# Attention with a gated feed-forward layer: where the PV and denominator groups stand in TensorE's order

## The chip, the cores and the metric

The kernel runs on one NeuronCore of one Trainium2 chip. The metric is the device time in microseconds (us), a median over runs of the same program. The profiled execution has a time of its own, and the working below is made against that one.

## What is computed

The reference is a layer in two halves. The first normalizes x, makes queries from it and keys and values from a context, does masked attention in 16 heads of 32 channels, and adds the result times a gate. The second normalizes again, rounds to 8-bit floating point, multiplies by a 1024 x 1024 matrix and adds that times a second gate. Cut to what matters:

```python
# x, ctx: (8, 512, 1024); mask: (8, 1, 1024), all float32
q, k, v = Wq @ layernorm(x) + bq, Wk @ ctx + bk, Wv @ ctx + bv     # per batch, 16 heads of 32
dot  = (q.T @ k) / sqrt(32);  mask2 = mask.T * mask                # per head, 1024 x 1024
amap = softmax(mask2 * dot - (1 - mask2) * 1e6, axis=-1) * mask2
x = x + tanh(g0) * (amap @ v)
y = layernorm(x)
x = x + tanh(g1) * (fp8(y * s) / s) @ (fp8(W2 * s1) / s1)
```

## The kernel before

The kernel has two parts. The first, up to about 630 us, turns the weights, makes q, k and v for all eight batches and writes them to memory. The second, from there to the end, is the attention with the feed-forward half. The change lies in the second.

**Tiling.** The second part goes over 32 quads. A quad is four heads of one batch, 128 channels in all. The work of a quad is cut into 64 slots (NSLOT). Slot k of quad n handles head h = k % 4, block j of 128 keys and half th of 512 queries. Two score products are made for each slot. `scores` (matmul on line 701) writes a tile of 128 keys x 512 queries into one of three banks s_bank, for the exponential. `scores_for_max` (line 714) writes a tile of 128 queries x 512 keys into one of three banks x_bank, from which VectorE takes the row maxima (`maximum`, line 871). The maxima have to be known before the exponentials of their half start, so this second product runs 19 slots ahead, partly for the next quad.

**Engines.** ScalarE takes the exponential of a score tile (line 807) into probs, a ring of PR = 4 blocks with 4 heads each, and makes the copies out of PSUM. `times_v` (line 727) multiplies a block of 4 heads by v: four heads stand side by side as tiles of 32 columns in the one bank o_bank, and sixteen blocks c belong to a quad, eight to each half. GpSimd adds pairs of blocks (`add_pair`, line 970), and `denominators` (line 738) sums them over the keys with a matrix of ones into the one bank d_bank, eight groups r a quad, also as tiles of 32 columns. Each group of four such products appears as eight matmul instructions in the trace. VectorE also carries the small steps of the next stages: `negate_max` after slots 18 and 50, `invert` after slots 20 and 51, `add_ffn` (line 929) after 14 and 28, and the steps of the second normalization and the rounding, as placed by these two lines:

```python
NORM_AT = {36: 2, 37: 3, 39: 4, 40: 5, 44: 6, 45: 7, 53: 9, 56: 10, 60: 11}
NORM_AT_2 = {0: 12, 3: 13, 6: 14}
```

Steps 2 and 3 are line 908, step 6 is line 917, step 7 line 919, step 9 line 92, step 10 line 95, step 11 line 97, step 12 line 99, step 13 line 102, step 14 line 103.

**Order.** The order of work on each engine is written out by hand. TensorE's `period(n, p)` goes through the slots; in each it issues `scores` and `scores_for_max`, then, at some slots, groups of PV and denominators, and at others jobs that take a bank of x_bank as well:

```python
F_JOBS = {10: "turn_y8", 13: "ffn0", 24: "max1", 27: "ffn1", 54: "max0"}
```

Each job or tile takes the next of the three banks x_bank in turn, and waits (`wait_bank`) until the user three places before is done; a score tile waits (`s_bank_freed`) for the exponential that reads its bank. Each engine works in its written order, so a wait holds up all behind it. Two periods, of an even and an odd quad, make up the body of a loop, with the first and last quads written out.

**Chains across engines.** `invert` of the half before stands after slot 20 on VectorE. Its result goes out by `move_inv` of the SyncE queue (to memory and back, spread over partitions), behind which `load_tm` and then `set_max(n, 1)` stand in the same queue; the score of slot 32 waits for that last one.

Of the kernel before, what the change touches and what calls it, by code (L numbers as in the profile page):

```python
# [28 lines left out]
def counted(value):  # L29


    return not isinstance(value, int) or value > 0


def flamingo_gated_layer(nc, x, ctx, mask, g_xattn, g_ffn, Wq, bq, Wk, bk, Wv, bv, W2, scale, scale1, out):
# [7 lines left out]
    SJ = S // P  # L43
# [20 lines left out]
    with ctxs:  # L64
# [480 lines left out]
        with ExitStack() as at:  # L545
# [71 lines left out]
            def real(n):  # L617

                return not isinstance(n, int) or 0 <= n < NQ

            def loads_of_parity(m, p):

                return 8 * (m - p) + 16

            def maxima_at(n, k):

                return (n + 1, 1, k - XLEAD) if k >= XLEAD else (n, 0, k + NSLOT - XLEAD)
# [64 lines left out]
            with nc.Block() as block:  # L692
                @block.tensor
                def _(pe):
                    def scores(n, p, k):
                        th, j, h = k // 32, k % 32 // QH, k % QH
                        if j == 0 and h == 0:
                            pe.wait_ge(max_set, 16 * (2 * n + th + 1))
                        if counted(NSLOT * n + s_bank_freed(k) + 1):
                            pe.wait_ge(exp_done, NSLOT * n + s_bank_freed(k) + 1)  # L700
                        nc.tensor.matmul(s_bank[S_BANK_OF[k]][:, :], k_st[p][0:KS, h, j * P:(j + 1) * P],  # L701
                                         q_st[p][0:KS, th, h, :], start=True, stop=True).then_inc(scores_ready, 1)
# [6 lines left out]
                    def scores_for_max(n, k, m, p, i):  # L709
                        th, h, tc, sh = tile_of_max(i)  # L710
                        if i == 0:
                            pe.wait_ge(stacked, 16 * STACK_DMAS * (m + 1))
                        wait_bank(n, "tile", k)
                        nc.tensor.matmul(x_bank_of("tile", k)[:, :], q_st[p][0:KX, th, h, tc * P:(tc + 1) * P],  # L714
                                         k_st[p][0:KX, h, sh * HALF:(sh + 1) * HALF],
                                         start=True, stop=True).then_inc(x_ready, 1)

                    def times_v(m, p, c):
                        th, j = c // SJ, c % SJ
                        if c == 0:  # L720
                            pe.wait_ge(v_loaded[p], loads_of_parity(m, p))
                        if j == 0:
                            if counted(2 * m + th):
                                pe.wait_ge(o_copied, 2 * m + th)
                        pe.wait_ge(exp_done, NSLOT * m + QH * (c + 1))
                        for h in range(QH):
                            last = nc.tensor.matmul(o_bank[D * h:D * (h + 1), :], v_t[p][:, j, D * h:D * (h + 1)],  # L727
                                                    probs[:, c % PR, h, :], start=(j == 0), stop=(j == SJ - 1))
                        last.then_inc(pv_done, 1)

                    def denominators(m, r):
                        th, i = r // 4, r % 4
                        if i == 0:
                            if counted(2 * m + th):
                                pe.wait_ge(den_copied, 2 * m + th)
                        pe.wait_ge(pair_done, QH * SJ * m + QH * (r + 1))
                        for h in range(QH):
                            last = nc.tensor.matmul(d_bank[D * h:D * (h + 1), :], ones[:, :], pair_sum[:, r % 2, h, :],  # L738
                                                    start=(i == 0), stop=(i == 3))
                        last.then_inc(den_done, 1)  # L740

                    def turn_max(n, k, m, th):
                        pe.wait_ge(negmax_done, 3 * (2 * m + th + 1))
                        wait_bank(n, f"max{th}", k)
                        nc.tensor.matmul(x_bank_of(f"max{th}", k)[:, 0:P], neg_max[:, :], ident_r[:, :], start=True,
                                         stop=True).then_inc(max_turned, 1)

                    def turn_y8(n, k, m):
                        pe.wait_ge(norm_done, NORM_STEPS * (m + 1))
                        wait_bank(n, "turn_y8", k)  # L750
                        turned = x_bank_of("turn_y8", k)[:, :].bitcast(BF16)
                        for kc in range(KC):
                            last = nc.tensor.transpose(turned[:, kc * P:(kc + 1) * P], y8[:, kc * P:(kc + 1) * P],
                                                       ident_b[:, :])
                        last.then_inc(y8_turned, 1)

                    def ffn(n, k, m, half, kcs):
                        if 0 in kcs:
                            pe.wait_ge(y8_copied, m + 1)
                            wait_bank(n, f"ffn{half}", k)  # L760
                        for kc in kcs:
                            last = nc.tensor.matmul(x_bank_of(f"ffn{half}", k)[:, :], y8_t[:, kc, :],  # L762
                                                    w2q[:, kc, half * HALF:(half + 1) * HALF],
                                                    start=(kc == 0), stop=(kc == KC - 1))
                        if KC - 1 in kcs:
                            last.then_inc(ffn_done, 1)

                    def period(n, p):
                        for k in range(NSLOT):
                            m, odd, i = maxima_at(n, k)  # L770
                            if real(n):
                                scores(n, p, k)
                            if real(m):
                                scores_for_max(n, k, m, (p + odd) % 2, i)
                            if k % 4 == 3:
                                if k >= 7 and real(n):
                                    times_v(n, p, (k - 7) // 4)
                                if k < 7 and real(n - 1):
                                    times_v(n - 1, 1 - p, 15)
                            if k % 8 == 3:  # L780
                                if k >= 19 and real(n):
                                    denominators(n, (k - 19) // 8)
                                if k < 19 and real(n - 1):
                                    denominators(n - 1, 6 + k // 8)
                            if k == 10 and real(n - 2):
                                turn_y8(n, k, n - 2)
                            if k == 24 and real(n):
                                turn_max(n, k, n, 1)
                            if k == 54 and real(n + 1):
                                turn_max(n, k, n + 1, 0)  # L790
                            for half, at_ in ((0, 13), (1, 27)):
                                if k in (at_, at_ + 1) and real(n - 2):
                                    ffn(n, at_, n - 2, half, range(4 * (k - at_), 4 * (k - at_) + 4))

                    run(pe, period)

                @block.scalar
# [319 lines left out]
```

## Time and profile before

| | us |
|---|---|
| median of 3 runs | 2907.09 (2902.08 to 2907.44) |
| time of the profiled execution | 2906.41 |
| span in its trace | 2904.3 |
| TensorE matmul busy | 2677.0 (92%) |
| VectorE busy | 2115.2 (73%) |
| ScalarE busy | 1450.8 (50%) |
| GpSimd busy | 1720.9 (59%) |

An engine's busy time is the union of its instructions' times. Matmuls are pipelined, so the start of one to the start of the next is what a matmul costs, not its own duration. In the timeline PE is TensorE's matmuls, PEld its weight loads, DVE VectorE, ACT ScalarE, POOL GpSimd, and SPq the queue of SyncE.

### The profile page before, as it was taken

The page shows a single profiled execution, that of the slowest core. Times are in us where ns is not written, and L with a number is a line of the kernel's source. Part 1 is how long each engine was busy: PE and PEld are TensorE (multiplying, and loading weights), DVE is VectorE, ACT ScalarE, POOL GpSimd, SP SyncE. Part 2 cuts the span into 40 slices and gives each one's busy share as a digit, 9 for nine tenths or more (in the row PEclk, how much of TensorE's full clock was granted, in tenths as well). Part 3 has the DMA queues.
Part 4 walks back from the last instruction along what each step waited for, and adds up shares of the span by engine and source line. Part 5 has one row for each costly group of instructions (what it writes and reads, how often), then busy time and mean ns, then how long its engine had stood idle before and what let it go on. Part 6 is the DMA issues. An engine that isn't in the chain of part 4 may idle for free. (4 is left out here: it accounts for less than half of the span.)

```text
span 2904.3 us, 51876 instructions
## 1 busy us (share of the span) xinstructions
PE 2677.0 (92%) x13364; PEld 1389.4 (48%) x13425; DVE 2115.2 (73%) x3314; ACT 1450.8 (50%) x2574; POOL 1720.9 (59%) x1265
## 2 busy tenths in 40 slices
PE   5999999969999999999999999999999999989995
PEld 4888888734444434443444444444444344434441
DVE  5666677466787878787778787777877787878873
ACT  3333333315555555555555555555555555555553
POOL 2333334416776767666667676666766676666764
PEclk8999999969999999999999999999999999999998
DMA  6766766553333333333333333434343433333301
GB/s 211 245 220 236 248 217 231 188 105 69 76 76 77 76 77 76 77 76 77 76 77 84 75 83 77 89 76 92 76 91 74 87 76 77 76 77 76 76 27 38
DMA packets 208376, 307.54 MB, mean 106 GB/s; under 512 B 41240, under 2 KB 108888, under 8 KB 208064
## 3 DMA queue, kind: packets, MB, share of 16 engines
q1 hardware_dynamic: 195920, 265.80, 37.7%
q10 hardware_dynamic: 12144, 38.02, 3.7%
q8 instruction: 141, 2.31, 0.4%
q14 instruction: 171, 1.40, 0.2%
HBM read 200.09 MB, written 102.11 MB: 104 GB/s over the span
## 5 line engine op out<-in xcount | busy, mean ns | idle before, releaser
L970 POOL TENSOR_TENSOR pair_sum<-probs 128x512 f32<-128x512 f32 x1024 | 1354.0, 1353 | 677.0 <-ACT probs L807 677.0
L871 DVE TENSOR_REDUCE part_max<-x_bank 128x1 f32<-128x512 f32 x2048 | 1309.6, 682 | 499.8 <-PE x_bank L714 487.5
L807 ACT ACTIVATE probs<-s_bank 128x512 f32<-128x512 f32 x2048 | 1122.0, 601 | 916.9 <-PE s_bank L701 909.3
L714 PE MATMUL x_bank<-k_st,q_st 98*128 98x512 f32 x2048 | 884.8, 436 | 92.2 <-DVE part_max L871 53.9
L701 PE MATMUL s_bank<-q_st,k_st 100*128 100x512 f32 x2048 | 905.2, 444 | 54.9 <-issue 34.5
L701 PEld LDWEIGHTS s_bank<-q_st,k_st 100*128 100x128 f32 x2048 | 393.6, 193 | 547.6 <-issue 282.3
L727 PE MATMUL o_bank<-probs,v_t 128*32 128x512 f32 x4096 | 562.6, 622 | 0.0
L714 PEld LDWEIGHTS x_bank<-k_st,q_st 98*128 98x128 f32 x2048 | 398.8, 195 | 335.0 <-DVE part_max L871 225.9
L738 PE MATMUL d_bank<-pair_sum,ones 128*32 128x512 f32 x2048 | 295.2, 607 | 13.7 <-issue 12.9
L321 POOL TENSOR_TENSOR stage_lo<-stage,stage_hi 128x512 fp32r<-128x512 f32 x128 | 186.6, 1480 | 123.3 <-ACT stage_hi L391 122.8
L391 ACT ACTIVATE stage_hi<-stage 128x512 fp32r<-128x512 f32 x128 | 79.8, 632 | 192.0 <-DVE stage L475 141.8
L738 PEld LDWEIGHTS d_bank<-pair_sum,ones 128*32 128x32 f32 x2048 | 70.3, 112 | 197.4 <-issue 173.9
L309 POOL TENSOR_TENSOR rstd<-ve,neg_half 128x4 f32<-128x4 f32 x8 | 14.6, 1829 | 250.5 <-DVE ve L506 250.5
L727 PEld LDWEIGHTS o_bank<-probs,v_t 128*32 128x32 f32 x4096 | 81.5, 109 | 157.0 <-issue 102.9
L979 POOL TENSOR_TENSOR y<-o_raw,inv_b 128x1024 f32<-128x1024 f32 x32 | 76.1, 2379 | 108.6 <-DMA inv_b<-inv_scr 108.6
L762 PE MATMUL x_bank<-w2q,y_t 128*128 128x512 bf16 x451 | 119.5, 385 | 8.1 <-issue 4.9
L447 PE MATMUL bank<-c_hi,w_hi_k 128*128 128x512 f32 x256 | 100.3, 392 | 14.6 <-DVE c_lo L458 14.6
L408 ACT ACTIVATE stage<-stage,sm_now 128x512 f32<-128x512 f32 x64 | 45.4, 722 | 121.1 <-DVE stage L471 120.3
L471 DVE TENSOR_TENSOR stage<-bank,bias_v 128x512 f32<-128x512 f32 x64 | 43.5, 690 | 84.2 <-PE bank L447 83.5
L447 PE MATMUL bank<-c_lo,w_hi_k 128*128 128x512 f32 x256 | 101.6, 397 | 0.0
L447 PE MATMUL bank<-w_hi_v,c_hi 128*128 128x512 f32 x256 | 101.3, 396 | 0.0
L447 PE MATMUL bank<-w_hi_v,c_lo 128*128 128x512 f32 x256 | 101.2, 396 | 0.0
(98 smaller groups left out, 2235.1 us busy)
## 6 DMA issues: line engine op xcount, KB each, us to landing
k_st<-k_scr SPq DMA_DIRECT2D x96, 512.0 KB
q_st<-q_scr SPq DMA_DIRECT2D x192, 256.0 KB
c_raw<-in_ctx_dram ACTq DMA_DIRECT2D x32, 512.0 KB, 7.3
x_raw<-in_x_dram ACTq DMA_DIRECT2D x32, 512.0 KB, 6.0
k_scr<-stage_hi SPq DMA_DIRECT2D x64, 256.0 KB, 2.4
k_scr<-stage_lo SPq DMA_DIRECT2D x64, 256.0 KB, 2.6
v_scr<-stage SPq DMA_DIRECT2D x64, 256.0 KB, 2.7
q_scr<-stage_hi SPq DMA_DIRECT2D x64, 256.0 KB, 2.1
```

What stands on the lines that cost most here:

```text
L321: nc.gpsimd.tensor_tensor(stage_lo[:, e % STG], stage[:, g % STG], stage_hi[:, e % STG].bitcast(F32), ALU.subtract).then_inc(qk_lo, 1)
L391: nc.scalar.activation(stage_hi[:, e % STG], stage[:, g % STG], ACT.Copy).then_inc(qk_hi, 1)
L447: last = nc.tensor.matmul(acc, a, m, start=(cb == 0 and n == 0), stop=(cb == CB - 1 and n == 2))
L701: nc.tensor.matmul(s_bank[S_BANK_OF[k]][:, :], k_st[p][0:KS, h, j * P:(j + 1) * P], q_st[p][0:KS, th, h, :], start=True, stop=True).then_i ...
L714: nc.tensor.matmul(x_bank_of("tile", k)[:, :], q_st[p][0:KX, th, h, tc * P:(tc + 1) * P], k_st[p][0:KX, h, sh * HALF:(sh + 1) * HALF], sta ...
L727: last = nc.tensor.matmul(o_bank[D * h:D * (h + 1), :], v_t[p][:, j, D * h:D * (h + 1)], probs[:, c % PR, h, :], start=(j == 0), stop=(j = ...
L738: last = nc.tensor.matmul(d_bank[D * h:D * (h + 1), :], ones[:, :], pair_sum[:, r % 2, h, :], start=(i == 0), stop=(i == 3))
L762: last = nc.tensor.matmul(x_bank_of(f"ffn{half}", k)[:, :], y8_t[:, kc, :], w2q[:, kc, half * HALF:(half + 1) * HALF], start=(kc == 0), st ...
L807: nc.scalar.activation(probs[:, c % PR, h, :], s_bank[S_BANK_OF[k]][:, :], ACT.Exp).then_inc(exp_done, 1)
L871: nc.vector.tensor_reduce(part_max[:, th, sh, at:at + 1], x_bank_of("tile", k)[:, :], AX, ALU.max).then_inc(max_done, 2)
L970: nc.gpsimd.tensor_tensor(pair_sum[:, r % 2, h], probs[:, a, h], probs[:, a + 1, h], ALU.add).then_inc(pair_done, 1)
L979: nc.gpsimd.tensor_tensor(y[:, :], o_raw[:, :, :].rearrange("p a t -> p (a t)"), inv_b[:, :, :].rearrange("p a t -> p (a t)"), ALU.mult).t ...
```

## The change

At every eighth slot (k % 8 == 3), TensorE issues two PV groups and then one denominator group. Before, it issued one PV group at every fourth slot and the denominator group behind every second of them. The PV group of each even block c thereby moves four slots later, from between slots 8i+7 and 8i+8 to behind slot 8i+11; that of each odd block, and the denominators, stay at their slots. The blocks 14 and 15 of a quad are now both done in the period of the next quad. The three banks s_bank, the three banks x_bank, the ring of probs, all other engines' programs and all transfers are as before.

```diff
@@ -772,12 +772,12 @@
                                 scores(n, p, k)
                             if real(m):
                                 scores_for_max(n, k, m, (p + odd) % 2, i)
-                            if k % 4 == 3:
-                                if k >= 7 and real(n):
-                                    times_v(n, p, (k - 7) // 4)
-                                if k < 7 and real(n - 1):
-                                    times_v(n - 1, 1 - p, 15)
                             if k % 8 == 3:
+                                for c in ((k - 11) // 4, (k - 7) // 4):
+                                    if k >= 11 and real(n):
+                                        times_v(n, p, c)
+                                    if k < 11 and real(n - 1):
+                                        times_v(n - 1, 1 - p, 2 * SJ + c)
                                 if k >= 19 and real(n):
                                     denominators(n, (k - 19) // 8)
                                 if k < 19 and real(n - 1):
```

## Rows read from the trace of the kernel before

**Rows 1.** The page: busy times, and the granted TensorE clock in 40 slices.

```profile
PE 2677.0 (92%) x13364; PEld 1389.4 (48%) x13425; DVE 2115.2 (73%) x3314; ACT 1450.8 (50%) x2574; POOL 1720.9 (59%) x1265
...
PEclk8999999969999999999999999999999999999998
```

**Rows 2.** Groups of instructions, 900 to 2800 us: count, busy us, mean ns, idle before.

```profile
L871 DVE TENSOR_REDUCE part_max<-x_bank 128x1 f32<-128x512 f32 x1728 | 1106.5, 681 | 403.3 <-PE x_bank L714 392.3
```

**Rows 3.** Timeline, TensorE, slots 32 to 41 of one period: start us, duration us, instruction.

```profile
1503.04 0.49 PE L701 MATMUL s_bank<-q_st,k_st 100*128 100x512 f32 x1 [0.50 <-DMA q_st<-max_rows]
1503.37 0.39 PE L714 MATMUL x_bank<-k_st,q_st 98*128 98x512 f32 x1
...
1505.10 1.06 PE L727 MATMUL o_bank<-probs,v_t 128*32 128x512 f32 x8
1505.98 1.04 PE L738 MATMUL d_bank<-pair_sum,ones 128*32 128x512 f32 x8
1506.95 0.50 PE L701 MATMUL s_bank<-q_st,k_st 100*128 100x512 f32 x1
1507.29 0.40 PE L714 MATMUL x_bank<-k_st,q_st 98*128 98x512 f32 x1
...
1508.70 0.39 PE L714 MATMUL x_bank<-k_st,q_st 98*128 98x512 f32 x1
1509.02 1.07 PE L727 MATMUL o_bank<-probs,v_t 128*32 128x512 f32 x8
1510.02 0.50 PE L701 MATMUL s_bank<-q_st,k_st 100*128 100x512 f32 x1
...
1511.19 0.50 PE L714 MATMUL x_bank<-k_st,q_st 98*128 98x512 f32 x1 [0.19 <-DVE part_max L871]
```

**Rows 4.** Timeline, VectorE and ScalarE, in the same slots; x4 is four in one line.

```profile
1503.87 2.48 DVE L871 TENSOR_REDUCE part_max<-x_bank 128x1 f32<-128x512 f32 x4 [1.41 <-PE x_bank L714]
...
1507.49 2.07 ACT L807 ACTIVATE probs<-s_bank 128x512 f32<-128x512 f32 x4 [0.58 <-PE s_bank L701]
```

**Rows 5.** One period: us, busy of PE, PEld, DVE, ACT, POOL; clock, DMA.

```profile
1533.50:1603.90 70.40, 64.58 (x348) 28.59 (x346) 56.99 (x92) 39.44 (x72) 50.30 (x38) 1.00 0.41 87
```

**Rows 6.** TensorE's own waits, 900 to 2800 us: total us, times, longest.

```profile
PE x_bank L714 <- DVE part_max L871: 45.5, 96, 1.0
```

**Rows 7.** Groups of instructions, 900 to 2800 us: VectorE's other work.

```profile
L97 DVE TENSOR_TENSOR y<-y,big 128x1024 f32<-128x1024 f32 x27 | 57.7, 2138 | 0.0
...
L908 DVE BATCH_NORM_STATS2 st<-res 128x6 f32<-128x512 f32 x54 | 37.2, 689 | 8.1 <-POOL res L985 7.6
L103 DVE TENSOR_TENSOR y<-y,isnan 128x1024 bf16<-128x1024 bf16 x27 | 37.1, 1376 | 0.0
...
L917 DVE TENSOR_TENSOR rss<-rs,scl 128x1 f32<-128x1 f32 x27 | 29.0, 1074 | 0.0
L92 DVE TENSOR_SCALAR big<-y 128x1024 uint32<-128x1024 uint32 x27 | 27.0, 1001 | 0.0
...
L919 DVE SCALAR_TENSOR_TENSOR nb<-mv,rss 128x1 f32<-128x1 f32 x27 | 19.3, 716 | 0.0
```

**Rows 8.** Timeline, VectorE: invert, and the reductions behind it.

```profile
1349.21 0.24 DVE L896 RECIPROCAL inv_c<-den_c 128x16 f32<-128x16 f32 x1
...
1350.21 1.87 DVE L871 TENSOR_REDUCE part_max<-x_bank 128x1 f32<-128x512 f32 x3
```

**Rows 9.** Timeline, TensorE, at a turn of the loop: slots 0 and 3.

```profile
1319.55 0.49 PE L701 MATMUL s_bank<-q_st,k_st 100*128 100x512 f32 x1 [2.87 <-issue]
...
1328.42 1.93 PE L738 MATMUL d_bank<-pair_sum,ones 128*32 128x512 f32 x6 [1.94 <-issue]
```

**Rows 10.** Timeline of TensorE at slot 7 of another period, and the windows about it.

```profile
1399.92 0.80 PE L714 MATMUL x_bank<-k_st,q_st 98*128 98x512 f32 x1 [0.90 <-DVE part_max L871]
1400.64 1.94 PE L727 MATMUL o_bank<-probs,v_t 128*32 128x512 f32 x8
...
1400.00:1406.80 6.80, 6.80 (x25) 3.56 (x25) 4.84 (x7) 1.79 (x3) 3.29 (x3) 0.50 1.05 181
```

## The prediction, made before the change was run

> **What bounds the kernel now.** I read the page first: TensorE is busy 92% of the span [rows 1]. A busy TensorE is not yet the bound, so the second view is the groups of instructions in the steady attention stage (900 to 2800 us). 1728 maxima in 1900 us are 27 periods of 64 slots, 70.4 us a period [rows 2]. The third view is the timeline of eight plain slots, 32 to 39, of one period [rows 3]. The reader is to see three paces there. TensorE issues the max matmuls of three slots from 1507.29 to 1508.70, so a slot takes it 0.47 us, half of it for the score and half for the max. VectorE needs more: four reductions fill 2.48 us, of which the first shows 0.69, so the following ones come every 0.60 us [rows 4]. ScalarE does four exponentials in 2.07, one every 0.49 us [rows 4]. So between the groups of PV and denominators TensorE runs faster than VectorE, by 0.13 us a slot, and can do so only until the three banks of x_bank are full. During the groups TensorE fills no bank of x_bank and VectorE catches up. VectorE has 57.0 of 70.4 us of work in one period, TensorE 64.6 [rows 5]: TensorE is the bound on average, but the hand-over through three banks decides inside each run of slots. Direct waits of TensorE for a reduction are small today, 45.5 us in 27 periods, the longest 1.0 us [rows 6].
>
> **The part that is taken away.** The change moves one PV group of each eight slots, from between slots 7 and 8 (mod 8) to slot 11, where a PV group and a denominator group already stand. The number of instructions is the same. What it removes is one entry and one exit. From the timeline [rows 3]: the lone PV group begins at 1509.02 and the next score at 1510.02, 1.00 us; the entry costs 1509.02 - 1508.70 = 0.32 in place of 0.24, and the pair after the exit 1507.29 - 1506.95 = 0.34 in place of 0.24. The lone group is thus worth 1.00 + 0.08 + 0.10 = 1.18 us of TensorE. A group that follows another costs 1505.98 - 1505.10 = 0.88. No row shows PV behind PV; PV behind PV could cost from 0.88 (as the row of PV then denominators) to 1.00 (the row of PV then score). I take 0.87 to 0.88, since the shapes of both operands are the same in both. **The gain is 1.18 - 0.87 = 0.31 us per eight slots**, 2.5 us a period, 79 us over 32 periods, if nothing else moves.
>
> One rule bears on this. The Trainium skill, "TensorEngine Tiling (Array Packing)", Key Properties, says that changing the tiling mode drains TensorE. The rows agree in kind, with 0.3 us for the pair of changes, and by that rule alone the time would fall by the 79 us. The same page, PSUM Bottleneck, speaks against the change: tiling speeds up TensorE and not the emptying of PSUM, which may become the bound.
>
> **The part that is added.** Take a run of eight slots with the time at zero when its first score starts. X(j), the max matmul of slot j of the run, starts at 0.34 + 0.47 j if nothing holds it. Its reduction starts 0.50 us after (1503.37 to 1503.87), then one every 0.60, each 0.69 long. X(j) needs the bank of X(j-3), so it can't start before 0.34 + 0.50 + 0.69, some 0.06 for the hand-over (an estimate), and 0.60 (j-3). The wait is, rounded, 0.13 j - 0.55 + e, where e is VectorE's other work that stands before tile j-3 of the run. In a plain run e is nothing and X(7) waits 0.36 us: this alone eats the 0.31. Today the lone group stands after j = 3, and 1.18 us are added to TensorE's side for all later j, so plain runs never wait. ScalarE's side is X's form with 0.49: score(7) would be held to about 3.2 us where it starts at 3.4, so it stays covered. GpSimd's pair sums start after the exponential of the slot behind the joint group, as today, and their denominators one group later (0.87 us) hold neither add_pair up, which waits for the exponential anyway, nor the ring of four probs: times_v of an even c comes five slots before its place is written again (line by line: c at slot 4c+11, the place at 4c+16).
>
> VectorE's other work makes the waits. From its groups [rows 7], less about 0.08 of overlap each: line 97 costs 2.06, line 917 1.0, line 919 0.63, line 908 0.61, line 92 0.93, line 103 1.3; invert costs 1.0 (1349.21 to 1350.21 [rows 8]). Today's wait behind the lone group (j of 4 and more) is the same formula less 1.18, so a run adds W = 0.13 j - 0.55 + e, but no more than 1.18, and gives back 0.31: **a run's loss lies between -0.31 and +0.87**. The upper end is plain: where VectorE is late anyway, a wait fills the place of the group that leaves, and the joint group behind is 0.87 longer. The eight runs of a period, named by their first slot:
> - 4: line 103 stands after slot 6. Today the max of slot 7 already waits in front of the lone group (0.90 at 1399.92 [rows 10]) and slot 10 again; afterwards the same lateness is waited for once. Bounds as above, taken 0.0.
> - 12: X(4) takes the bank of ffn0, which add_ffn has to empty; today the lone group lies between. An estimate of 0.46, so +0.15.
> - 20: invert stands after slot 20, so X(4), slot 24, waits 1.0 - 0.03, and turn_max takes a bank behind it, some 0.2: full, +0.87.
> - 28: the score of slot 32 waits today (0.50 us at 1503.04 [rows 3]) for a chain that starts with invert at slot 20 and goes through three transfers. The chain's length from slot 20 is unchanged, so slot 32 starts where the chain ends, 0.0.
> - 36: line 908 after slots 36 and 37: X(5) waits 1.22 + 0.10 = 1.3, full; but the formula leaves 0.1 of it today, and the max of slot 41 waits more than that already (0.19 directly at 1511.19, and the loading of its weights behind the wait [rows 3]). I take 0.3 for it, +0.60.
> - 44: lines 917 and 919: X(5) 1.63 + 0.10 = 1.7, full, +0.87.
> - 52: line 92 after slot 53: X(5) 0.93 + 0.10 = 1.0, less some 0.2 at turn_max of slot 54 today: +0.55.
> - 60: line 97 in front of X(4), which is slot 0: 2.06 - 0.03 = 2.0, full, +0.87.
>
> The sum is **+3.9 us a period**. At every second period the loop turns, and TensorE sits idle for its instructions, 2.87 us at slot 0 and again in the denominators of slot 3 (1319.55 and 1328.42 [rows 9]). VectorE catches up there in both kernels, and the PV group taken out in front of that gap comes back behind it, so I count half of run 60's loss there: 3.5 us on the mean of two periods. Some 30 of the 32 periods have all this work: 30 x 3.5 = 105 us. The edges I leave at nothing.
>
> **The clock.** The granted clock is full in almost all of the stage (the row PEclk [rows 1]); besides the loop turns it fell after the wait of 0.90 us for a reduction at 1399.92, to 0.50 for 6.8 us [rows 10], in which a PV group shows 1.94 us in place of 1.06. That is the lower of the two levels, 1.2 GHz, and before it TensorE had issued only scores and waits, no group. Runs of eight slots have longer stretches of just that kind. I count five per period with about 1 us or more of waiting (slots 0, 10, 24, 41, 48), where today there is about one in two periods. A fall of 6.8 us costs at most 3.4 us and less where VectorE sets the pace. Bounds: no new fall, 0 us; a fall at each, 5 x 1.7 x 30 = 255 us. The nearest row is the one that fell, yet most waits pass without a fall, so I take one and a half falls of 1 us a period, 45 us.
>
> The sum against the profiled execution's own time, 2906.4 us (span 2904.3): 2906.4 + 105 + 45 = 3056. The median shown, 2907.1, is 0.7 above it, which I disregard.
>
> **The rivals.**
> - Heavy throttling, slower still: the long waits bring a fall of the clock nearly each time. For it: the fall of rows 10. Against: 96 direct waits in 27 periods [rows 6], and the clock's row is full nearly throughout [rows 1]. 4 falls a period at 1.5 us more: 2906 + 105 + 180 = 3191; chance 0.15.
> - The waits come at half of their size, since the extra steps of VectorE overlap better or some gaps are taken up by ffn: 2906 + 50 = 2956; chance 0.11.
> - Faster: the 0.31 us count in full, since VectorE's lateness is caught up in the joint group and isn't a wait of TensorE. This decides if the wait in an average run stays under 0.31 us, that is if VectorE's reductions follow at under 0.59 us in a run with no other work, or if the three banks free earlier than I read. For it: TensorE is busy 92% and VectorE idles a fifth. Against: five of eight runs carry 0.6 us or more of other work in their first half. 2906 - 79 = 2827; chance 0.07.
> - Nothing: the gain and the waits cancel, or the period hangs on the chain of set_max and the loop turn alone: 2907; chance 0.04. That the change doesn't do what it says is not open: the order of the groups is written out in the period.
>
> **How the numbers follow.** The forecast's chance is 0.63, with a range of its own from 2990 (waits alone, somewhat smaller) to 3120 (twice the clock's share and some more). For 8 in 10 I go down to 2950, which takes in the half-sized waits, and up to 3150, which takes a part of the heavy throttling. About 0.2% (6 us) is what a measurement of this kernel can tell from no change; faster 0.07, same 0.04, slower 0.89.
>
> **What would show it.** TensorE's groups: 24 matmuls in a row, the second PV 0.88 us behind the first. Direct waits of the max matmuls for reductions well above 45.5 us in the same number of periods, standing at slots 0, 10, 24, 40, 48 and 56, each 0.5 to 1.7 us. The slots 12 to 19 take almost the same time as today. VectorE's idle time moves into the joint groups. Granted clock below today's, with new falls inside periods. Wrong would be: those waits near 0.3 us, or a period's growth that stands in the exponentials, the pair sums or the chain to slot 32.

## The result

The changed kernel takes 3135.98 us (median of 4 runs, 3124.96 to 3148.68) against 2904.59 us beside it: a ratio of 1.080, 95% interval 1.075 to 1.086. It is slower by 231 us, where +150 us was forecast. 3136 us lies in the range of 8 in 10 (2950 to 3150), but above the forecast's own range (2990 to 3120), and is nearer to the 3191 of heavy throttling (55 us away) than to the 3056 of the forecast (80 us away). The profiled execution took 3124.96 us. TensorE, VectorE and the granted clock on the page of the changed kernel, which answer to [rows 1]:

```profile
PE 2756.7 (88%) x13364; PEld 1448.5 (46%) x13425; DVE 2111.3 (68%) x3314; ACT 1445.9 (46%) x2574; POOL 1717.8 (55%) x1265
...
PEclk8999999798899998899999988899988999899988
```

The instructions are the same ones. VectorE's busy time has not moved (2111 against 2115 us); its share has only sunk with the longer span. TensorE's busy time has grown by 80 us at the same number of matmuls, and the clock row has many more eights. Its mean is 0.923 in place of 0.958.

TensorE's own waits in the changed kernel, 900 to 2700 us (in us in total, times, longest):

```profile
PE x_bank L714 <- DVE part_max L871: 133.2, 180, 1.6
PE s_bank L701 <- issue: 42.2, 12, 3.8
PE s_bank L701 <- DMA q_st<-max_rows: 19.5, 15, 2.3
```

The direct wait for a reduction was 45.5 us in 27 periods [rows 6]; now it is 133.2 us in 23. A period is 77.8 us long, on the mean of 26, and was 70.6 in the same count. Both are read from the first max matmul of one quad to that of the next.

**A run of eight, as predicted.** The timeline of TensorE in the changed kernel, slots 44 to 51 of one period and the score behind them:

```profile
1673.10 0.50 PE L701 MATMUL s_bank<-q_st,k_st 100*128 100x512 f32 x1
...
1674.85 0.39 PE L714 MATMUL x_bank<-k_st,q_st 98*128 98x512 f32 x1
1675.27 0.50 PE L701 MATMUL s_bank<-q_st,k_st 100*128 100x512 f32 x1
1676.27 0.50 PE L714 MATMUL x_bank<-k_st,q_st 98*128 98x512 f32 x1 [0.50 <-DVE part_max L871]
1676.61 0.40 PE L701 MATMUL s_bank<-q_st,k_st 100*128 100x512 f32 x1
1677.49 0.53 PE L714 MATMUL x_bank<-k_st,q_st 98*128 98x512 f32 x1 [0.48 <-DVE part_max L871]
...
1679.67 2.68 PE L727 MATMUL o_bank<-probs,v_t 128*32 128x512 f32 x16
1682.18 1.03 PE L738 MATMUL d_bank<-pair_sum,ones 128*32 128x512 f32 x8
1683.14 0.50 PE L701 MATMUL s_bank<-q_st,k_st 100*128 100x512 f32 x1
```

VectorE in the same slots:

```profile
1673.94 0.69 DVE L871 TENSOR_REDUCE part_max<-x_bank 128x1 f32<-128x512 f32 x1 [2.19 <-PE x_bank L714]
1674.55 1.06 DVE L917 TENSOR_TENSOR rss<-rs,scl 128x1 f32<-128x1 f32 x1
1675.53 0.68 DVE L871 TENSOR_REDUCE part_max<-x_bank 128x1 f32<-128x512 f32 x1
1676.13 0.71 DVE L919 SCALAR_TENSOR_TENSOR nb<-mv,rss 128x1 f32<-128x1 f32 x1
1676.76 3.07 DVE L871 TENSOR_REDUCE part_max<-x_bank 128x1 f32<-128x512 f32 x5
```

The reader is to follow the banks. The first reduction ends at 1674.63, the step of line 917 pushes the second to 1675.53, and it ends at 1676.21: the max matmul of slot 48, which needs that bank, starts at 1676.27. Line 919 does the same to slot 49: 1677.44, 1677.49. Nothing else is late by more than 0.2 us. Then the PV groups, which cost 0.88 us each at full clock, take 1682.18 - 1679.67 = 2.51 us for two. The windows about this stretch (us; busy of PE, PEld, DVE, ACT, POOL; clock; DMA) say why:

```profile
1672.00:1678.00 6.00, 4.99 (x25) 2.35 (x17) 4.06 (x7) 4.17 (x7) 3.69 (x3) 0.99 0.01 1
1678.00:1681.30 3.30, 3.30 (x13) 1.24 (x15) 3.10 (x9) 1.68 (x4) 1.29 (x2) 0.51 0.00 0
1681.50:1688.00 6.50, 5.73 (x31) 2.89 (x24) 4.19 (x7) 3.30 (x7) 3.65 (x3) 1.00 0.17 49
```

Right behind the two waits the clock is at its lower level, 1.2 GHz, and the largest group falls into it. With the clock up, the same joint group of the same kernel, here in slot 59, is 1.74 us for the two PV groups and 2.72 until the next score:

```profile
1688.66 1.92 PE L727 MATMUL o_bank<-probs,v_t 128*32 128x512 f32 x16
1690.40 1.04 PE L738 MATMUL d_bank<-pair_sum,ones 128*32 128x512 f32 x8
1691.38 0.50 PE L701 MATMUL s_bank<-q_st,k_st 100*128 100x512 f32 x1
```

**Run by run.** From the first score of each run to that of the next, the mean of 26 periods, in us:

| run of slots | before | changed | difference | predicted |
|---|---|---|---|---|
| 4 to 11 | 9.35 | 10.37 | +1.02 | 0.0 |
| 12 to 19 | 8.74 | 8.84 | +0.10 | +0.15 |
| 20 to 27 | 8.42 | 9.36 | +0.94 | +0.87 |
| 28 to 35 | 8.89 | 9.49 | +0.60 | 0.0 |
| 36 to 43 | 7.91 | 8.76 | +0.85 | +0.60 |
| 44 to 51 | 7.89 | 10.05 | +2.16 | +0.87 |
| 52 to 59 | 7.54 | 8.25 | +0.71 | +0.55 |
| 60 to 3 | 11.59 | 12.52 | +0.93 | half of 0.87 |
| sum | 70.3 | 77.6 | +7.3 | +3.5, and 1.5 for the clock |

Thirty-one periods of 7.3 us are 226 of the 231 us.

### The profile page after: what moved, and what is told of

Its sections match the earlier page's. It is cut to its first block and busy times, and to the rows that moved or that the text cites. A ratio compares the mean times of both kernels' runs of the same rounds, so it can differ in the third digit from the quotient of the medians.

```text
span 3123.2 us, 51890 instructions
## 1 busy us (share of the span) xinstructions
PE 2756.7 (88%) x13364; PEld 1448.5 (46%) x13425; DVE 2111.3 (68%) x3314; ACT 1445.9 (46%) x2574; POOL 1717.8 (55%) x1265
## 5 line engine op out<-in xcount | busy, mean ns | idle before, releaser
L714 PE MATMUL x_bank<-k_st,q_st 98*128 98x512 f32 x2048 | 920.2, 453 | 220.6 <-DVE part_max L871 179.5
L714 PEld LDWEIGHTS x_bank<-k_st,q_st 98*128 98x128 f32 x2048 | 408.8, 200 | 522.2 <-DVE part_max L871 390.1
L727 PE MATMUL o_bank<-probs,v_t 128*32 128x512 f32 x4096 | 598.1, 710 | 0.0
L701 PEld LDWEIGHTS s_bank<-q_st,k_st 100*128 100x128 f32 x2048 | 403.4, 197 | 374.3 <-issue 256.5
L738 PE MATMUL d_bank<-pair_sum,ones 128*32 128x512 f32 x2048 | 277.7, 599 | 2.8 <-issue 1.8
L727 PEld LDWEIGHTS o_bank<-probs,v_t 128*32 128x32 f32 x4096 | 120.1, 123 | 300.9 <-issue 191.5
L813 ACT ACTIVATE o_raw<-o_bank 128x512 f32<-128x512 f32 x64 | 38.3, 598 | 149.7 <-PE o_bank L727 149.7
L447 PE MATMUL bank<-c_hi,w_lo_k 128*128 128x512 f32 x256 | 101.6, 397 | 0.0
L447 PE MATMUL bank<-x_hi,w_lo_q 128*128 128x512 f32 x256 | 101.3, 396 | 0.0
```

The lines of the kernel that those rows point to most:

```text
L447: last = nc.tensor.matmul(acc, a, m, start=(cb == 0 and n == 0), stop=(cb == CB - 1 and n == 2))
```

## The experiments

Each was timed beside the kernel before, whose median was 2898.7 to 2899.9 us there. Numbers by slot or by run of slots are means over the same 26 periods as in the table above.

### Is it the pair of PV groups?

Two PV groups stay together, and the denominators stand alone between. TensorE then changes as often between the two kinds of matmul as before. In the first form the denominators come four slots later, and ScalarE's copies of them with them:

```diff
                             if k % 8 == 3:
                                 for c in ((k - 11) // 4, (k - 7) // 4):
...
-                                if k >= 19 and real(n):
-                                    denominators(n, (k - 19) // 8)
-                                if k < 19 and real(n - 1):
-                                    denominators(n - 1, 6 + k // 8)
+                            if k % 8 == 7:
+                                if k >= 23 and real(n):
+                                    denominators(n, (k - 23) // 8)
+                                if k < 23 and real(n - 1):
+                                    denominators(n - 1, 6 + k // 8)
```

> The two PV groups stay together at slots k % 8 == 3, as in the changed kernel, but the denominator group stands alone at k % 8 == 7 (four slots later than before, and the two copies of its bank on ScalarE also four slots later, after slots 16 and 48). So TensorE enters and leaves the groups as often as in the kernel before, while PV stands behind PV as in the changed one. Theory (runs of eight slots without a group are what costs): runs are four slots again, VectorE catches up twice in eight slots, so the time is near the kernel before, 2905 to 2960 us, with few falls of the clock; by the rows 1.4 us a period more at most, since the short group is 0.1 us shorter and the denominators come later. Rival (two PV groups behind each other are slow in themselves, on their one bank): well above 3000. Rival (number of changes between the two tilings is all that counts): 2905, the same as before.

Measured: 3029.7 us, ratio 1.043 (1.039 to 1.046). No theory named this. The trace shows a cause that lies in the edit and not in the pair, at least for a part. With the denominators later, GpSimd's next pair sums wait for them, and run at another time:

```profile
1644.91 5.01 POOL L971 TENSOR_TENSOR pair_sum<-probs 128x512 f32<-128x512 f32 x4 [5.62 <-PE d_bank L738]
...
1647.51 1.21 DVE L881 TENSOR_TENSOR row_max<-part_max 128x16 f32<-128x16 f32 x1
1648.75 1.21 DVE L886 TENSOR_SCALAR neg_max<-row_max 128x16 fp32r<-128x16 f32 x1
```

The two small steps of `negate_max` take 1.21 us each under the pair sums; in the changed kernel they take 0.18 and 0.17. The run of slots 52 to 59, with the second of the two `negate_max` just before it, takes 11.00 us, in place of 7.54 before and 8.25 in the changed kernel. Run 36 to 43 is longer too (9.54 in place of 7.91), and that was not followed up. So the second form puts the denominators four slots earlier instead, where no chain starts later:

```diff
+                            if k % 8 == 7:
+                                if k >= 15 and real(n):
+                                    denominators(n, (k - 15) // 8)
+                                if k < 15 and real(n - 1):
+                                    denominators(n - 1, 7)
```

> As the run with the denominators apart, but four slots earlier than in the kernel before instead of later: two PV groups at k % 8 == 3, the denominator group alone at k % 8 == 7, all copies where they were. No chain starts later than before. Theory (what costs is the run of eight slots without a group): the time is that of the kernel before, 2885 to 2930 us, the max matmuls wait no more than there, and the clock falls as seldom. Rival (PV behind PV is slow in itself): 3000 or more, with the second PV group more than 0.88 us behind the first. Rival (the loss of the earlier run with denominators apart came from the pair of PV groups, not from its later copies): 3000 again.

Measured: 2932.6 us, ratio 1.012 (1.009 to 1.014), mean clock 0.960: just above the theory's 2930 us and far from both rivals' 3000. The kernel's groups:

```profile
1513.73 1.92 PE L727 MATMUL o_bank<-probs,v_t 128*32 128x512 f32 x16
1515.59 0.50 PE L701 MATMUL s_bank<-q_st,k_st 100*128 100x512 f32 x1
...
1517.66 1.06 PE L738 MATMUL d_bank<-pair_sum,ones 128*32 128x512 f32 x8
1518.66 0.50 PE L701 MATMUL s_bank<-q_st,k_st 100*128 100x512 f32 x1
```

Two PV groups cost 1.86 us until the next score, as PV and denominators do (1.85 in [rows 3]). Seven of the eight runs are within 0.1 us of the kernel before. The eighth, that of slots 28 to 35, is 1.3 us longer in the periods behind a turn of the loop, mostly at slot 31, behind which the next score waits for the chain of set_max (22.4 us in total in place of 11.4). The cause is the one found for run 28 of the changed kernel, further below. PV behind PV is not what costs.

### How much is the clock?

The score matmul of the slots in which TensorE waits long is issued several times into its own bank, so that the waits are filled and nothing else changes:

```diff
+                    FILL = {0: 5, 10: 4, 24: 3, 40: 2, 41: 2, 48: 3, 49: 2, 56: 3}
...
-                        nc.tensor.matmul(s_bank[S_BANK_OF[k]][:, :], k_st[p][0:KS, h, j * P:(j + 1) * P],
-                                         q_st[p][0:KS, th, h, :], start=True, stop=True).then_inc(scores_ready, 1)
+                        for _ in range(FILL.get(k, 0) + 1):
+                            last = nc.tensor.matmul(s_bank[S_BANK_OF[k]][:, :], k_st[p][0:KS, h, j * P:(j + 1) * P],
+                                                    q_st[p][0:KS, th, h, :], start=True, stop=True)
+                        last.then_inc(scores_ready, 1)
```

> The changed kernel, in which the score matmul of slots 0, 10, 24, 40, 41, 48, 49 and 56 is issued several times over (5, 4, 3, 2, 2, 3, 2 and 3 times more, 0.24 us each) into its own bank, the last one counting. The repeats fill most of the waits for VectorE that stand at these slots: 24 more matmuls, 5.7 us more of TensorE work a period. Theory (half of the loss is the clock that falls after long waits): the falls vanish for the most part, granted clock back from 0.92 to about 0.95, and although TensorE has more to do the time falls from 3136 to 3020 to 3080 us. Rival (the waits are the whole loss, and the half clock costs nothing because VectorE sets the pace there): 3136 to 3180 us. Rival (the clock falls because groups are rare, not because TensorE waits): granted clock stays at 0.92, time 3140 or more.

Measured: 2992.6 us (1.031, 1.028 to 1.034), 143 us less than the changed kernel, with 24 more matmuls in every period. The mean clock is 0.966, above that of the kernel before. The trace's record of the clock has 17 stretches at the lower level in the attention stage, where the changed kernel has 88 and the kernel before 22. Slots 48 to 51 in this kernel, and the groups behind them:

```profile
1626.27 1.20 PE L704 MATMUL s_bank<-q_st,k_st 100*128 100x512 f32 x4
1627.30 0.47 PE L718 MATMUL x_bank<-k_st,q_st 98*128 98x512 f32 x1
1627.61 0.87 PE L704 MATMUL s_bank<-q_st,k_st 100*128 100x512 f32 x3
1628.52 0.50 PE L718 MATMUL x_bank<-k_st,q_st 98*128 98x512 f32 x1
...
1630.14 1.92 PE L731 MATMUL o_bank<-probs,v_t 128*32 128x512 f32 x16
1631.88 1.04 PE L742 MATMUL d_bank<-pair_sum,ones 128*32 128x512 f32 x8
```

The max matmul of slot 49 is 1.22 us behind that of slot 48 in both kernels: VectorE sets that time, filled or not. But the PV groups behind take 1.74 us in place of 2.51. So the theory held, and the effect is larger than was expected (3020 to 3080 us): some 143 of the 231 us came with the fallen clock, and 88 us are left for the waits, where 105 had been predicted. The falls inside periods are gone altogether: from 900 to 2700 us all 13 stretches at the lower level start in slots 63 to 3, about a turn of the loop, where 45 of the changed kernel's 67 start elsewhere, 26 of them in slots 43 to 51 and 15 in slots 10 and 11. And run by run the filled kernel is longer than the kernel before by -0.01, 0.11, 0.87, -0.16, 0.47, 0.86, 0.71 and 0.13 us (in the order of the table), 3.0 us in all: close to the column that was predicted without the clock. The split is a rough one: the repeats also cost where no wait covers them, the filled kernel has fewer falls than the kernel before, and TensorE's waits for instructions changed a little (33.1 us in place of 42.2).

### Pace of the reductions, or the long steps between them?

Three pairs, each an order of before and the changed order with the same part made light. First all of it: reductions, rounding steps, statistics, add_ffn and pair sums on 64 columns.

```diff
+            LT = 64
...
-                        nc.vector.tensor_reduce(part_max[:, th, sh, at:at + 1], x_bank_of("tile", k)[:, :], AX,
+                        nc.vector.tensor_reduce(part_max[:, th, sh, at:at + 1], x_bank_of("tile", k)[:, 0:LT], AX,
...
-                            ins = f8_step(step - 9, y[:, :], big[:, :], y8[:, :], isnan[:, :])
+                            ins = f8_step(step - 9, y[:, 0:LT], big[:, 0:LT], y8[:, 0:LT], isnan[:, 0:LT])
```

> The order of before, with VectorE and GpSimd made light: the reductions read 64 of 512 columns, the rounding steps, the statistics and add_ffn 64 columns of their 512 or 1024, the pair sums 64 columns. This leaves out most of the maxima, of the second half's arithmetic and of the denominators. It is the base for the next run. Its own waits for VectorE go, so by the rows of before 4 to 6 us a period less: 2720 to 2790 us.

> The changed order with the same light VectorE and GpSimd (the same parts left out). Theory: the change is worth 0.31 us per eight slots on TensorE, and VectorE's lateness alone turns it round; with VectorE light no max matmul waits, and the run is faster than the light kernel of the order before, by 45 to 80 us (six and a half to eight times 0.31 us in 31 periods; the chain to slot 32 may hold back the runs of slots 20 and 28). Granted clock as in the light base. Rival (the joint group costs by itself, by its length, its bank or the clock): same as the light base or slower.

Measured: 2810.9 us (0.967 of before; 2797.9 to 2819.7) and 2843.1 us (0.978; 2829.8 to 2850.8). The base lies above its 2790 us, and the changed order is 32 us slower where 45 to 80 us faster was expected. Both expectations fell, the second for a reason that the waits show. In the changed order, TensorE's waits from 900 to 2700 us are:

```profile
PE x_bank L715 <- DMA q_st<-qx_scr: 51.7, 13, 4.4
PE s_bank L702 <- DMA q_st<-max_rows: 50.1, 26, 2.9
PE s_bank L702 <- issue: 41.6, 12, 3.9
PE d_bank L739 <- issue: 5.3, 7, 1.5
PE x_bank L715 <- DVE part_max L872: 0.3, 1, 0.3
```

The wait for reductions is gone (0.3 us), and two others have come, for the transfers that stack the next quad (needed at slot 19) and for set_max (slot 32). In the base they are 33.1 and 30.1 us. What the change gives in a run is given back at slots 19 and 32, and at slot 19 with a fallen clock. Between those places the gain is there, in most runs: the run of slots 36 to 43 takes 6.65 us in place of 6.98, and that of 20 to 27 7.63 in place of 7.96 in the periods behind a turn. Run 52 gains only 0.16 us, and run 44 nothing (7.01 and 6.98): the score of slot 48 there waits for ScalarE, which copies the bank of the denominators first. **The 0.31 us were right, as 0.33 measured where nothing else holds**; a kernel whose VectorE is light does not get them, because the next bounds are close. The time is the rival's, and so is a part of the cause: without any lateness of VectorE the changed order still has the lower clock (0.933 against 0.948, with 55 stretches at the lower level against 39).

Second, only the long steps light, reductions and pair sums full (the same edits of the steps, without the first of the two above):

> The order of before, with VectorE's steps other than the reductions light: statistics, rounding steps and add_ffn work on 64 of their 512 or 1024 columns. This leaves out most of the second half's arithmetic. Reductions, pair sums and all else are full. The base for the next run; some 2 us a period less than before, 2820 to 2860 us.

> The changed order with the same light steps (the same parts left out). This parts the two causes in the prediction: the pace of the reductions alone, 0.36 us of wait in a plain run of eight against 0.31 us of gain, and the long steps. Theory (the long steps are most of the loss): 0 to 60 us over the light base, in place of 231. Rival (the pace in a long run, with the clock's falls, is the cause): 150 us or more over the base.

Measured: 2853.2 and 2981.7 us, 128 us apart: between the two expectations. The steps did not become as light as meant. Line 97 on 64 columns still takes 1125 ns, where it takes 217 ns in the kernel whose pair sums are light as well: beside full pair sums it waits for GpSimd. Invert and lines 917 and 919 were left as they are. The changed order waits 84.2 us for reductions here, for the most part behind those very steps: slots 10, 24, 48 and 56 take 0.4 to 1.1 us more than in the base.

Third, the reductions on 256 columns, all steps full:

> The order of before, with each reduction over 256 of its 512 columns. This leaves out half of the maxima. Steps are full. The base for the next run: 2740 to 2830 us.

> The changed order with the half reductions (the same part left out). A reduction takes some 0.35 us, less than TensorE's slot of 0.47, so the pace of a run can hold nothing up, and only the long steps can. Theory (the long steps are most of the loss): still 80 us or more over its base, up to 180 with the clock. Rival (the pace is the cause): at or under its base.

Measured: 2834.9 and 2937.4 us, 102 us apart. A reduction takes 0.42 us, less than a slot of TensorE (0.47), and still the changed order waits for a reduction 43.5 us in 900 to 2700 us, its base not once. So the pace is not needed for a loss: without it 102 of the 231 us remain. Not all of them need be the long steps' own, since the light pair, with neither pace nor long steps, is 32 us apart as well.

### Does the place of a step decide?

In the changed order, VectorE's steps are put at other slots, mostly nearer to the joint group. No work is left out.

```diff
-                    NORM_AT = {36: 2, 37: 3, 39: 4, 40: 5, 44: 6, 45: 7, 53: 9, 56: 10, 60: 11}
-                    NORM_AT_2 = {0: 12, 3: 13, 6: 14}
+                    NORM_AT = {35: 2, 37: 3, 39: 4, 40: 5, 41: 6, 47: 7, 51: 9, 56: 10, 58: 11}
+                    NORM_AT_2 = {0: 12, 3: 13, 4: 14}
...
-                            if k == 20 and real(n - 1):
+                            if k == 19 and real(n - 1):
                                 invert(n - 1, 1)
...
-                            if k == 51 and real(n):
+                            if k == 50 and real(n):
                                 invert(n, 0)
```

> The changed order on TensorE, and VectorE's steps moved for it (steps 2, 3, 4, 5, 6, 7, 9, 10, 11 after slots 35, 37, 39, 40, 41, 47, 51, 56, 58; step 14 after slot 4; the inverts after slots 19 and 50). Theory: five of the seven us that a period is longer than before come from steps that stand early in a run of eight slots; 2930 to 3010 us, with fewer falls of the clock than 88, since the long waits are shorter. Rival (the pace of the reductions in a run of eight slots is the cause, wherever the steps stand): 3080 to 3140.

Measured: 2901.1 us over ten runs, ratio to the kernel before 1.000 (0.998 to 1.001). **All of the 231 us are gone** by moving VectorE's steps, though the TensorE order is that of the change. The theory had named 2930 us as its lowest. The waits for reductions:

```profile
PE x_bank L714 <- DVE part_max L871: 54.8, 81, 1.4
```

Slot 49 passes in 0.49 us in place of 1.23 to 1.35, slot 0 in 0.61 in place of 2.40 in the periods without a turn of the loop. This is the strongest evidence that VectorE's lateness in the long runs is the cause. It does not show that the slot in the run is all that counts, for the steps also became shorter where they now stand: line 97 takes 1.21 us in place of 2.13, line 917 0.16 in place of 1.07, line 92 0.68 in place of 1.00 (line 95 1.54 in place of 1.05). How much each did was not parted. And the gain of 0.31 us a run doesn't come through here either: the clock is at its lower level in 41 stretches (22 before, 88 in the changed kernel), slots 11, 43 and 51 still take 3.96, 3.47 and 3.85 us, and slot 8 has a new wait (2.04 us in place of 0.56). The same idea in the order of before, steps moved to stand in front of groups:

```diff
+                    NORM_AT = {36: 2, 37: 3, 38: 4, 40: 5, 43: 6, 44: 7, 53: 9, 55: 10, 59: 11}
+                    NORM_AT_2 = {0: 12, 4: 13, 7: 14}
```

> The order of before on TensorE; on VectorE the steps of the normalization and rounding and the two inverts stand at other slots, chosen so that the long ones fall in front of a group (steps 4, 6, 7, 10 and 11 after slots 38, 43, 44, 55 and 59, steps 13 and 14 after slots 4 and 7, invert of the half before after slot 18 in place of 20). Theory (VectorE's lateness within a run is a wait of TensorE, and the place of a step decides): 2.5 us a period less by the rows' recurrence, 2810 to 2860 us, waits for reductions below 20 us in place of 42. Rival (the waits only move, VectorE's total is what counts): 2895 to 2910.

Measured: 2905.6 us, 1.001 (0.999 to 1.003): a miss, the rival's value. The slots had been chosen by the prediction's formula, stepped through all slots of a period, with each step's duration as it was before. VectorE and GpSimd in this kernel at slots 58 and 59:

```profile
1589.82 1.82 DVE L95 TENSOR_SCALAR big<-big 128x1024 f32<-128x1024 f32 x1
...
1593.96 1.21 DVE L97 TENSOR_TENSOR y<-y,big 128x1024 f32<-128x1024 f32 x1
```

```profile
1586.87 5.89 POOL L970 TENSOR_TENSOR pair_sum<-probs 128x512 f32<-128x512 f32 x4 [2.22 <-ACT probs L807]
```

Line 95 now lies under the pair sums and takes 1.82 us, not 0.92; line 97 lies behind them and takes 1.21, not 2.13. The max matmul of slot 59 waits 1.11 us for it, and turn_y8 at slot 10 waits 31.7 us in all. Run 52 to 59, with lines 95 and 97 in it, takes 8.92 us in place of 7.54; this and 0.8 us in runs 4 and 12 cancel the 2.1 us that the five other runs gain. A last try had the longer group at slots k % 8 == 7 (denominators as in the second form above, but PV left at every fourth slot) and steps moved for it.

> The order of before with the denominator group behind the PV group of slots k % 8 == 7 instead of 3 (so four slots earlier), and VectorE's steps moved for it (steps 2 to 7 after slots 38, 39, 42, 43, 44, 46, step 11 after slot 63, steps 12, 13 and 14 after slots 2, 4 and 5, add_ffn of the first half after slot 15, invert of the first half after slot 54). A try for a kernel better than both. Theory: the longer group stands where VectorE is latest, 3.4 us a period less than before by the recurrence, 2780 to 2840 us. Rival (VectorE's total counts, or the loop turn and the instructions' arrival take the gain): 2880 or more.

Measured: 2939.0 us, 1.012 (1.006 to 1.018), the rival's side as well. TensorE's waits, from 900 to 2700 us:

```profile
PE s_bank L701 <- issue: 57.9, 12, 6.7
PE o_bank L727 <- issue: 33.0, 13, 4.0
...
PE x_bank L714 <- DVE part_max L871: 7.3, 11, 1.8
```

The waits for reductions have all but gone, 7.3 us in place of 41.9, as the formula wanted. What took the gain is the rival's second half: TensorE waits 90.9 us for nothing that the profile shows (`issue`, as at the turns of the loop), in place of 44.7; slot 63 at a turn of the loop takes 7.1 us in place of 4.2, and the mean clock is 0.939. No version here beats the kernel before.

## Why the prediction was right, and where its sum was off

- **The gain, 0.31 us per run**: right in size, 0.33 in runs that nothing else holds, and PV behind PV costs the 0.87 to 0.88 that was taken (1.74 for two).
- **The waits.** Right in kind and place: they stand at slots 0, 10, 24, 40, 41, 48, 49 and 56. Runs 12, 20, 36 and 52 were predicted within 0.25 us. What was said of the cover of ScalarE, of the pair sums and of the ring of probs held but for one place: the score of slot 48 comes 0.65 us behind that of slot 47, not 0.47, where ScalarE has a copy in between. None of them has another wait of note in the changed kernel.
- **The clock: the term that was mis-sized.** It was taken as 45 us between bounds of 0 and 255, and is about 143. The prediction counted one and a half falls of 1 us a period. The changed kernel has 71 stretches at the lower level more than the filled one, 2.3 a period, and the 143 us make 2.0 us of each (an estimate from these two runs), so both factors were too small, the price most. The joint group was not in that price. A fall follows a wait late in a run, and the next thing on TensorE is three groups in a row, which run at half speed as far as the lower level reaches: slots 51 and 11 take 4.56 and 4.31 us, and 3.40 and 3.36 in the filled kernel. Against that kernel run 44 holds 1.3 us of this loss, run 4 1.0, runs 60 and 28 0.8 each and run 36 0.4. The rival of heavy throttling had the clock's share too high (180 us, by 4 falls a period); the outcome lies between it and the forecast.
- **Run 4**: the 0.0 was right without the clock, on the mean, and by luck. The wait in front of the lone group, read in one period, is there in every second period only: slot 7 takes 2.87 us in these and 1.56 in the periods behind a turn. So the run grows by 2.24 us behind a turn and shrinks by 0.19 in the others. The mean excess of 1.02 is that of the clock in slot 11, which takes 3.93 and 4.69 us in the two kinds of period and 3.36 in both where the waits are filled.
- **Run 60**: counting half of 0.87 for the turn of the loop was right in kind. With the turn the run is 0.4 us shorter than before, without it 2.27 longer. In the filled kernel these are 0.58 us less and 0.86 more, and +0.13 on the mean, so most of the measured +0.93 is the clock.
- **Run 28**: in the periods without a turn before them the chain to slot 32 ended as predicted, and the run is 0.2 us shorter. Behind a turn the score of slot 32 comes 14.44 us after that of slot 20 in place of 13.60, and the group of slot 35 falls into the lower clock: 1.4 us more. The prediction took the chain's length as fixed, and its first transfer was not: issued 2.56 us behind slot 20 in both kernels, the result of `invert` lands after 2.31 us on the mean in place of 1.46. The DMA view of one such place (2199.5 to 2201.5 us, the transfer issued at 2199.74) shows why; queue, packets, MB, share of 16 engines:

```profile
q1 hardware_dynamic: 144, 0.01, 4.6%
q8 instruction: 1, 0.02, 3.0%
```

A 16 KB packet of the instruction queue, about 1 us long, starts with the transfer, in each of the 13 periods behind a turn 0.05 to 0.18 us after its issue. In the kernel before, the packet comes 0.6 us or more ahead of it or not at all there, in the filled kernel not at all, and the transfer takes 1.46 us in both. By this reading the change moved the slots against the arrival of instructions, and that they meet here is chance. The run with the denominators four slots earlier has the same packet at the same place, and 2.26 us for the transfer.

- **The pace and the steps.** The prediction gave the pace alone 0.36 us of wait in a plain run. No run is plain enough to show it; the half reductions say that the steps do 102 us without it, and the pair with light steps that the pace, with the steps that stayed long, does 128. These two don't add up to 231 and needn't, since a lateness is waited for once, and each holds what the order costs without any lateness (32 us in the light pair).

On the rules that were weighed: PSUM Bottleneck of "TensorEngine Tiling (Array Packing)" in the Trainium skill, by which the emptying of PSUM may become the bound, agrees with the trace in so far as TensorE waits for the engine that empties the banks, 133.2 us in place of 41.9 in the same window; but a reduction takes 0.68 us in both kernels, and what made it late was mostly VectorE's other steps. The rule on changing the tiling mode, in Key Properties of the same page of the Trainium skill, agrees in kind, with 0.33 us, and decided nothing.

## What to carry to other kernels

When a faster engine is interrupted by blocks of other work, the blocks are where the slower one catches up. Before joining two of them, lay the slower engine's odd steps along the run between them and see which stand in its first half; move those first, for here that was worth the whole 231 us. Measure a moved step anew, since its duration moves with it. And price a wait of TensorE with what stands right behind it: if that is the largest block, a fallen clock makes much more of it (2.51 us in place of 1.74 for the two PV groups here).

## What was not expected of the hardware

Many of VectorE's steps on SBUF have no fixed duration beside a busy GpSimd. Under pair sums, an operation on 128 x 16 elements took 1.21 us in place of 0.18, line 95 on 128 x 1024 took 1.82 in place of 0.92, and line 917, on a single column, has a mean of 1.07 us in the kernel before and 0.15 where it was moved. Cutting line 97 to 64 of 1024 columns brought it from 2.13 to 1.13 us only, and to 0.22 where the pair sums were light too. GpSimd's pair sums lengthen too, 5.89 us for four in place of 5.01. The Trainium skill, "SBUF — State Buffer", section "SBUF: two separate sides", says that the two share a pair of ports under an exclusive lock, held for a whole instruction. The rows agree: the time added is about that of one pair sum or less. The full reductions, which read PSUM, kept their 0.68 us throughout, and so did the full statistics of line 908 (0.68 to 0.69). So for the others a measured duration holds only at its place, and this is a part of what the formula missed in the try that moved steps in the order of before.
